# Two softmax attentions of a 12-stage decoder: ones rows by DMA instead of a memset, the first sequence loaded by chunk and the other three in one span, keys and angles ahead of the norm

## What is computed

```python
q = apply_rope(q, sin, cos); k = apply_rope(k, sin, cos)     # after x @ wq, x @ wk
scores = einsum('bhqk,bhsk->bhqs', q, k) / sqrt(dk)
scores = where(causal, -inf, scores)
out = einsum('bhqs,bhsv->bqhv', softmax(scores), v) @ wo
```

```python
q = (x @ Wq).reshape(b, n, 32, 8); k, v = split(ctx @ Wkv, 2)
q = axial_rope(q, pos_map); k = axial_rope(k, ctx_pos_map)   # angle = pos * freqs
out = softmax(q @ k.T * scale) @ v ; out = out @ Wout + bout
```

## Time and profile before

| | |
|---|---|
| time of the kernel, median of 3 runs | 2011.71 us (2011.18 to 2017.87) |
| the profiled execution's own time | 2005.86 us |
| its span | 2004.0 us |
| TensorE clock granted over the span, mean | 0.809 of full speed |
| PE / DVE / ACT / POOL busy | 1119.7 / 1142.7 / 473.7 / 595.1 us |
| DMA queues, bytes moved | 196.51 MB, mean 98 GB/s |

### The profile page before, as it was taken

One profiled execution on the slowest core, in us unless ns is written; L12 is line 12 of the kernel. 1 busy time (PEld: TensorE's weight loads), 2 busy tenths in 40 slices (PEclk: granted clock), 3 DMA queues, 4 the chain that ended last, 5 costly groups with the idle time before them and its releaser, 6 DMA issues. The chain is left out here.

```text
span 2004.0 us, 21287 instructions
## 1 busy us (share of the span) xinstructions
PE 1119.7 (56%) x5620; PEld 707.5 (35%) x5620; DVE 1142.7 (57%) x1850; ACT 473.7 (24%) x881; POOL 595.1 (30%) x588
## 2 busy tenths in 40 slices
PE   5325536886054862552596704697566378537760
PEld 2202124664023640211354503575333034335540
DVE  5659974333354545998876694311357477463333
ACT  2143302221011444330211101332122266212220
POOL 0026614333620111661200081134302122043325
PEclk9659968998577886997798856899878599868985
DMA  6024335886307302331000011206500500357763
GB/s 203 2 85 147 104 106 167 261 263 188 94 8 147 45 2 87 130 121 63 0 0 1 0 16 27 85 1 181 174 8 2 170 21 3 121 160 213 220 191 102
DMA packets 146192, 196.51 MB, mean 98 GB/s; under 512 B 35056, under 2 KB 109954, under 8 KB 145484
## 3 DMA queue, kind: packets, MB, share of 16 engines
q1 hardware_dynamic: 109996, 144.47, 24.3%
q0 software_dynamic: 12608, 31.26, 5.9%
q10 hardware_dynamic: 23520, 19.93, 3.1%
HBM read 153.55 MB, written 41.75 MB: 97 GB/s over the span
## 5 line engine op out<-in xcount | busy, mean ns | idle before, releaser
L163 PE MATMUL psum<-w_ident,h 128*128 128x128 f32 x144 | 32.9, 423 | 188.3 <-DVE h L144 188.3
L453 PE MATMUL psum<-l0s_conv_out,w_ident 128*128 128x512 f32 x128 | 65.0, 632 | 83.4 <-DVE l0s_conv_out L550 83.4
L453 PE MATMUL psum<-l1s_conv_out,w_ident 128*128 128x512 f32 x128 | 65.6, 638 | 81.3 <-DVE l1s_conv_out L550 81.3
L1481 DVE TENSOR_REDUCE l3x_neg<-psum 128x2 f32<-128x512 f32 x128 | 80.9, 684 | 49.7 <-PE psum L1353 49.7
L163 PEld LDWEIGHTS psum<-w_ident,h 128*128 128x128 f32 x144 | 29.2, 224 | 191.7 <-DVE h L144 179.5
L175 ACT ACTIVATE hT<-psum 128x512 f32<-128x512 f32 x40 | 21.7, 595 | 310.4 <-PE psum L163 268.7
L933 PE MATMUL psum<-l0f_w_in,l0f_xT 128*128 128x352 f32 x224 | 79.1, 476 | 22.2 <-issue 12.4
L1456 ACT ACTIVATE l3x_work<-psum 128x512 f32<-128x512 f32 x128 | 72.5, 599 | 65.0 <-PE psum L1375 64.7
L152 POOL TENSOR_SCALAR rstd<-moments 128x8 f32<-128x8 f32 x12 | 2.9, 240 | 281.6 <-DVE moments L140 281.6
L933 PE MATMUL psum<-l3f_w_in,l3f_xT 128*128 128x192 f32 x256 | 64.5, 381 | 39.2 <-DMA l3f_w_in<-in_l3f_w_in 18.6
L419 POOL TENSOR_TENSOR l1s_xpad<-l1s_du,l1s_bc 128x1024 f32<-128x1024 f32 x32 | 75.2, 2352 | 32.5 <-DVE psum L546 32.4
(11 more groups left out here) (604 smaller groups left out, 3211.3 us busy)
## 6 DMA issues: line engine op xcount, KB each, us to landing
l0f_w_in<-in_l0f_w_in SPq DMA_DIRECT2D x56, 352.0 KB
l0s_bc<-l0s_scratch SPq DMA_DIRECT2D x16, 1024.0 KB, 5.1
l1s_bc<-l1s_scratch SPq DMA_DIRECT2D x16, 1024.0 KB, 5.2
l3f_w_in<-in_l3f_w_in SPq DMA_DIRECT2D x64, 192.0 KB
l0f_w_down<-in_l0f_w_down SPq DMA_DIRECT2D x56, 176.0 KB
l2f_w_in<-in_l2f_w_in SPq DMA_DIRECT2D x24, 352.0 KB
l3f_y_rows<-h SPq DMA_DIRECT2D x16, 512.0 KB, 6.8
l3f_y_rows<-l3f_y ACTq DMA_DIRECT2D x64, 128.0 KB
```

Source lines behind the costliest of these rows:

```text
L163: ins = nc.tensor.transpose(m.psum[:, at:at + P], m.h[:, t, k * P:(k + 1) * P], m.ident[:])
L453: ins = nc.tensor.matmul(m.pair(2 + c)[:, cols], lhsT=m.ident[:], rhs=rhs[:, cols], start=start, stop=stop, skip_group_check=True)
L1481: ins = nc.vector.tensor_reduce(self.neg[k % 2][:, :, hl], bank[:, 0:self.keys].rearrange("p (q k) -> p q k", q=self.maxima), AX_X, ALU.ma ...
```

## The change

- `Attention.gpsimd` no longer sets `packed["k"]`. A new constant `bf16_ones` (3 x 8192 words) is copied into the three ones rows of each side by DMAs that ACT issues as its first instructions of the stage (`scalar_ones`).
- `order` lists the tiles (x, c), x = 0 for q and 1 for k: q0, k0, q1, k1 in the self attention as before, and k0, q0, k1, q1 in the cross attention.
- `first_stored` becomes one semaphore for each chunk. SP stores chunk 0 of sequence 0, waits until it has landed and issues its 12 loads. Then it stores chunk 1, waits, and loads q; ACT loads k of chunk 1.
- The stores of the other sequences move behind these loads, and `SPANS` becomes sequence 0, then 1 to 3 together.
- In the cross attention PE projects `angle` and `k0` ahead of the norm's transposes, and DVE takes the angles out of PSUM while it waits for `rstd`.

```diff
 def norm_vector(m, dve, n, meanwhile=None):
...
     ins.then_inc(m.moments_ready, 1)
+    if meanwhile is not None:
+        meanwhile()
     dve.wait_ge(m.rstd_ready, n + 1)
...
-    SPANS = ((0, 1), (1, 2), (2, 4))
-    ONES = float(np.array([0x3F803F80], np.uint32).view(np.float32)[0])
+    SPANS = ((0, 1), (1, B))
...
+        self.order = [(x, c) for c in range(KD) for x in ((0, 1) if causal else (1, 0))]
...
-        for c in range(KD):
-            for x in range(2):
-                sp.wait_ge(self.split, KD * c + x + 1)
-                store(c, x, slice(0, S), self.first_stored)
-        for c in range(KD):
-            for x in range(2):
-                store(c, x, slice(S, T), self.rest_stored)
-        sp.wait_ge(self.first_stored, 16 * 2 * KD)
-        for c in range(KD):
-            self.load(sp, 0, c, 0)
+        for i, (x, c) in enumerate(self.order):
+            sp.wait_ge(self.split, i + 1)
+            store(c, x, slice(0, S), self.first_stored[c])
+            if i == 1:
+                sp.wait_ge(self.first_stored[0], 16 * 2)
+                sp.wait_ge(self.ones_ready, 16 * self.sides)
+                for y in range(2):
+                    self.load(sp, 0, 0, y)
+        sp.wait_ge(self.first_stored[1], 16 * 2)
+        self.load(sp, 0, 1, 0)
+        for x, c in self.order:
+            store(c, x, slice(S, T), self.rest_stored)
         sp.wait_ge(self.rest_stored, 16 * 2 * KD)
-        sp.wait_ge(self.ones_ready, 1)
         for i in range(1, len(self.SPANS)):
...
+    def scalar_ones(self, act):
+
+        for c in range(self.sides):
+            rows = slice(64 * c + self.rows, 64 * c + self.rows + 3)
+            act.dma_start(self.packed["k"][rows, :, :].bitcast(F32),
+                          self.m.dram["bf16_ones"].rearrange("p (h t) -> p h t", h=16)).then_inc(self.ones_ready, 16)
...
-        nc.gpsimd.memset(self.packed["k"][:].bitcast(F32), self.ONES).then_inc(self.ones_ready, 1)
...
         def _(pe):
-            norm_tensor(m, pe, n)
-            m.wait_weights(pe, tag)
...
-            if not self_attn:
+            if self_attn:
+                norm_tensor(m, pe, n)
+                m.wait_weights(pe, tag)
+            else:
+                m.wait_weights(pe, tag)
                 project(m, pe, jobs, "angle", lambda k: w("freq")[:], lambda k, cols: w("pos")[:, cols], 1)
...
+                project(m, pe, jobs, "k0", wcols(w("k"), 0), keys, kc)
+                norm_tensor(m, pe, n)
...
         def _(act):
+            a.scalar_ones(act)
             norm_scalar(m, act, j)
...
-            act.wait_ge(a.ones_ready, 1)
-            act.wait_ge(a.first_stored, 16 * 2 * KD)
-            for c in range(KD):
-                a.load(act, 0, c, 1)
+            act.wait_ge(a.first_stored[1], 16 * 2)
+            a.load(act, 0, 1, 1)
...
+            def angles():
+                jobs.wait_filled(dve, "angle")
+                ps = jobs.pair("angle")
+                o.mark(nc.vector.tensor_scalar(turns[0][:], ps, 0.25, None, ALU.add))
+                nc.vector.tensor_copy(turns[1][:], ps).then_inc(jobs.empty("angle"), 1)
+                dve.wait_ge(jobs.emptied["vector"], 1)
+                o.wait(dve)
+
+            norm_vector(m, dve, n, None if self_attn else angles)
```

More of the change, by code:

```diff
@@ L1205, in __init__ @@
                              "mixed_ready", "inv_ready", "whole_ready"))
-        self.first_stored, self.rest_stored = sem("first_stored"), sem("rest_stored")
+        self.first_stored, self.rest_stored = [sem(f"first_stored{c}") for c in range(KD)], sem("rest_stored")
         self.loaded = [sem(f"loaded{i}") for i in range(len(self.SPANS))]
@@ L1240, in head, with parts_of @@
         return b, 0, i, i
+    def parts_of(self, i):
+        x, c = self.order[i]
+        return self.parts[2 * c + x]
     def split_scalar(self, act, i, scale):
-        x, parts = self.rotated[i % 2], self.parts[i]
+        x, parts = self.rotated[i % 2], self.parts_of(i)
         act.wait_ge(self.rot_ready, i + 1)
@@ L1514, in softmax_attention @@
     a = Attention(m, tag, heads, causal)
-    scales = (a.hd ** -0.5, 1.0) * KD
+    scales = [(a.hd ** -0.5, 1.0)[x] for x, _ in a.order]
     names = [] if self_attn else ["angle"]
-    for c in range(KD):
-        names += [f"q{c}", f"q{c}s", f"k{c}", f"k{c}s"]
+    for x, c in a.order:
+        names += ["qk"[x] + str(c), "qk"[x] + f"{c}s"]
     jobs = Jobs(m, tag + "in", 2, [(x, "vector") for x in names] + [("v0", "scalar"), ("v1", "scalar")])
@@ L1553, in _ @@
             kc = KD if self_attn else 1
-            if not self_attn:
-                project(m, pe, jobs, "angle", lambda k: w("freq")[:], lambda k, cols: w("pos")[:, cols], 1)
-            for c in range(KD):
-                project(m, pe, jobs, f"q{c}", wcols(w("q"), c), hT, KD, turn=None if c else j)
-                project(m, pe, jobs, f"q{c}s", wcols(w("q"), KD + c), hT, KD)
-                project(m, pe, jobs, f"k{c}", wcols(w("k"), c), keys, kc)
-                project(m, pe, jobs, f"k{c}s", wcols(w("k"), KD + c), keys, kc)
+            if self_attn:
[3 more added lines that the diff above has]
+                m.wait_weights(pe, tag)
+                project(m, pe, jobs, "angle", lambda k: w("freq")[:], lambda k, cols: w("pos")[:, cols], 1)
+                project(m, pe, jobs, "k0", wcols(w("k"), 0), keys, kc)
+                norm_tensor(m, pe, n)
+            started = 0 if self_attn else 1
+            for i, (x, c) in enumerate(a.order):
+                rhs, chunks = (hT, KD) if x == 0 else (keys, kc)
+                for half, name in enumerate(("qk"[x] + str(c), "qk"[x] + f"{c}s")):
+                    if 2 * i + half >= started:
+                        project(m, pe, jobs, name, wcols(w("qk"[x]), KD * half + c), rhs, chunks,
+                                turn=j if 2 * i + half == started else None)
             src = m.hT if self_attn else m.ctxT[:].unsqueeze(1)
@@ L1611, in _ @@
             if not self_attn:
-                jobs.wait_filled(dve, "angle")
-                ps = jobs.pair("angle")
-                o.mark(nc.vector.tensor_scalar(turns[0][:], ps, 0.25, None, ALU.add))
-                nc.vector.tensor_copy(turns[1][:], ps).then_inc(jobs.empty("angle"), 1)
-                dve.wait_ge(jobs.emptied["vector"], 1)
                 for i in range(2):
@@ L1625, in turn @@
             def turn(i):
-                x = ("q", "k")[i % 2] + str(i // 2)
+                x = "qk"[a.order[i][0]] + str(a.order[i][1])
                 rotate(m, dve, jobs, x, x + "s", tables[0], tables[1], tmp,
```

9 lines of the change are left out of this document (4 added, 5 removed).

## The result

The changed kernel takes 2029.32 us (median of 4 runs, 2025.85 to 2032.47), the kernel before 2011.45 in the same set (4 runs, 1993.48 to 2017.87). The medians differ by 18 us. The ratio of the runs is 1.011, interval 1.0072 to 1.0148: slower by 1.1%. The prediction was 2007.3, range 1990 to 2024. Both the time and the sign are wrong.

The account below looks back on a forecast made before the run. It took twelve stages in a row, passing gains on one for one, with engines idle in l1a and l3x. l1a +6.0 and l3x -10.4 gave -4.4 against the median 2011.71: 2007.3 us, range 1990 to 2024.

Parts of the forecast that it names:

- Step 1: Norm in l1a and l3x: without GpSimd's memset DVE's eight instructions fall from 9.25 to 2.68 us; 6.5 us gained.
- Step 2: Front of l3x: angles and first key ahead of the norm start the rotation 11.2 us earlier, 6.5 from the memset.
- The sum: Forecast total over both attention stages: l1a +6.0 and l3x -10.4 us, together -4.4.
- Step 3: First sequence stored and loaded chunk by chunk: first score 7.1 us sooner in l1a, 7.5 in l3x.
- -18.7: Largest gain in us allowed for l3x: front 11.2 plus chunk by chunk 7.5.
- Step 4: Sequences 1 to 3 loaded together: PE's 17th (l1a) or 33rd (l3x) head waits for all 24 loads of 192 KB.
- R: Time of the 24 loads of 192 KB: taken as 37.5 us in l1a and 35 in l3x.
- the slower rival: Packed loads to one block of partitions don't overlap: +7.4 us (2019) to +23 (2035); chance 0.17.
- The 1.5 us for its clock: Allowance in l1a for PE having warmed up before the turned heads, chosen between nothing and 3.9 us.

Follow-up runs that it names:

- e2: Kernel before plus the front alone (ones by DMA, angles and k0 ahead of the norm in l3x), old stores, loads and spans; ratio to before 0.9899.
- e5: e2 with sequences 1 to 3 in one joint span; ratio to before 1.0111, l1a 187.7 us, l3x 238.4 us.
- e6: e2 with a span for each sequence; 1979.44 us, ratio to before 0.9842.
- e10: e6 with the two chunks of a block loaded in turn in l3x; median 1966.25 us, ratio to before 0.9809.
- e1: Changed kernel with the three spans of the kernel before (sequence 0, then 1, then 2 and 3); ratio to before 0.9956.
- e3: Changed kernel, joint wait kept, each 192 KB load cut into three of 64 KB, issued sequence by sequence; l1a 190.7 us, l3x 217.7 us.
- e4: e3's 72 loads, but each block's three sequences loaded one after the other; l1a 200.5 us, l3x 251.4 us.
- e7: Changed kernel with the big stores held back until all loads of sequence 0 have landed; l1a 195.5 us, l3x 238.0 us.
- e9: e3 with the two chunks of each block loaded in turn; l1a 195.9 us, l3x 228.7 us.
- e12: Changed kernel with a span for each sequence instead of the joint one; ratio to before 0.988.
- e13: e3 with a chunk's six blocks reordered so neighbours are often 32 or 64 partitions apart; 24-load replacement took 40.3 us in l1a, 43.1 in l3x.
- e8: Changed kernel with chunk 0's k loads issued by ACT beside SP's q loads; l1a 191.4 us, l3x 234.4 us.
- e11: Kernel before with a span for each sequence and nothing else changed; ratio to before 0.9866.

## Why the prediction was wrong

**Step 1, the memset: right.** 9.25 us became 2.67, and the transposes start 6.58 us earlier, for 6.5 predicted. The ones' DMA was hidden: no wait for it shows.

**Step 2, the front of l3x: right.** The rotation starts 12.3 us earlier, 11.2 predicted. What was missing is that the stage keeps only 6.5 (e2), as PE then waits longer for `neg_rows` beside the loads. The sum passed the shift on in full. It had read these waits as there "in l1a alone", while the kernel before has two in l3x as well, of 6.84 and 3.52 us.

**Step 3, chunk by chunk: direction right in l1a only, sizes wrong.** Predicted were 7.1 and 7.5 us sooner at the first score, from the change of order alone. In the kernels with the front and the old order (e2, e5, e6, e10; in l3x the first three) the first score is at +67.4 in l1a and +61.8 in l3x, in the mean. In the eight with the new order (after, e1, e3, e4, e7, e9, e12, e13) it is at +63.6 and +63.4. So the order gives 3.8 us in l1a. In l3x it gives nothing: the means say that it costs 1.6, but the two groups overlap (+60.7 to +62.7, and +61.5 to +64.3). Two terms fell. The twelve loads of chunk 1 with their landing were put at 5.7 and 6.3 us. They took 8.6 (616.76 to 625.32) and 13.8 (1565.08 to 1578.84). The rates of 183 and 161 GB/s came from stretches in which one load after another of both chunks was under way from two queues; twelve loads of one chunk are another case (that this is the reason isn't shown), and e7 shows that the big stores beside them aren't to blame. The other term is the stores of chunk 1 in l3x, landed at +49.75 where the working has +47.3. They stand behind twelve loads on SP's queue; with six of these moved to ACT's they landed 4.85 us sooner (e8). Together 7.5 + 2.4 make the 9.9 us by which the first score missed its -18.7.

**Step 4, where the 24 loads begin.** In l1a +69.57, predicted +67.2. In l3x +68.37, predicted +60.6. Beside the slow loads of chunk 1 the big stores took 16.5 us in l3x from their issue, priced at 10.7. But they landed 4.9 us behind the first score, where the working has 7.0 (l1a 5.6, working 6.5). So the price of the stores held, and the lateness is that of step 3.

**Step 4, R: the step that failed most.** In l1a 40.7 us against 37.5, 1.70 us for a load, taken as 1.56. In l3x 54.3 against 35, 2.26 us for a load, taken as 1.46. Over R as measured that is 115 and 86 GB/s, where 125 to 140 had been forecast. The l1a miss is within what the same loads spread by (e8 has 36.7 by the same count); the one in l3x is not. I extrapolated with the row's length, which put a load of 1536-byte rows near 1.5 us. e3 and e4 show that row length isn't what costs: with rows of 512 B alone, R is 35.0 or 67.6 in l3x by the order of the queue. The reading that fits is that a 192 KB load keeps one block of 8 partitions for its whole length and lets little of the next run, which is what the slower rival said. The runs show the price of such an order for pieces of 64 KB; for the 192 KB loads themselves it is argued. I gave it 0.17, as its evidence in the earlier trace rows (0.36 us for the first 512 B, 0.64 for the second) was clearest in l1a. The 0.407 and 0.943 us of l3x spoke for it just as much, and I took them as cover for a flat rate.

These terms give back the result. l1a: 6.0 + 2.4 + 3.2 = +11.6, measured +10.7. l3x: -10.4 + 7.8 + 19.3 = +16.7, measured +16.8. The rest in l1a is PE, 0.9 us faster behind the 17th head than taken. The 1.5 us for its clock in l1a had a wrong reading behind it: it was at full speed in the kernel before already ahead of 668.75 (0.99 and 1.00 in the two stretches above).

**Open.** Why neighbours 64 partitions apart (e9) are slower than neighbours 8 apart, why chunk 1's twelve loads are 5 us slower in l3x than in l1a, and what made the front of e11's l3x late. How much of e4's and e13's loss lies on the HBM side, which their orders change too, and by which part of the chip blocks collide, no run shows. That l3x keeps only part of its front's gain rests on one kernel (e2) and its waits.

## What to carry to other kernels

Loads that each fill few partitions are priced by what their neighbours in the queue fill, not by bytes: measure one pair of orders before merging them. Here the smaller pieces, in turn over the blocks, made one stage 19.9 us shorter than the same bytes in longer rows (in the other, 4.6 us), and a span for each sequence with the front alone was worth 1.6% where the change as made lost 1.1%. When an in-order engine meets a joint wait, the gain of everything ahead of it is lost unless the slowest load gets sooner too; price that wait first.

## What the runs showed of the hardware

- The same 72 loads of 64 KB into blocks of 8 partitions took 35.0 us with different blocks as neighbours and 67.6 with each block three times in a row; with 16 partitions 37.5 and 44.5. Each is one run, and the same 24 loads of 192 KB spread by 4 to 5 us between kernels.
- Loads into blocks of 8 partitions have a DMA share near 0.6 (0.60, 0.54, 0.62 in the stretches above), into blocks of 16 above 1.0, and yet e3 moves more bytes in l3x (146 against 135 GB/s), since there issuing doesn't bind it. A share over 1.0 was not a sign of a good rate: e4's 1.22 goes with 112 GB/s.
- SP issues a load every 0.47 us in l1a and every 0.36 in l3x when it never waits, so in e3's l1a the 64 KB loads from one queue go no faster than 139 GB/s.
- With six of twelve such loads moved to a second queue, the stores behind them landed 4.85 us sooner (e8). The Trainium skill (DMA: Bandwidth & Descriptors, Issuing engines are not separate DMA queues) says that a second issuing engine saves only the time of the issues. Here the stores went out 2.2 us sooner for that reason (+40.08, in the changed kernel +42.28) and landed 4.85 us sooner, and the first score, which needs all loads, came 4.45 us sooner, more than that rule gives. What gave the rest isn't shown.
